# Normalising attention sums through HBM instead of by transposes, in a fused attention and FP4 feed-forward kernel

## What is computed

```
q = rope((xn @ Wqa @ Wqb).reshape(b, s, 16, 8));  k, v from xn @ Wkva @ Wkvb, k = rope(k)
scores = einsum('bqhd,bkhd->bhqk', q, k) * 8**-0.5, causal mask
w = softmax(scores);  out = einsum('bhqk,bkhd->bqhd', w, v).reshape(b, s, 128)
x + out @ Wout + bout + fp4_linear(silu(fp4_linear(xn, w_gate)) * fp4_linear(xn, w_up), w_down)
```

## Time and profile before

| | |
|---|---|
| median of 3 runs | 821.9 us (819.39 to 822.25) |
| profiled execution | 822.47 us, its span 820.7 us |
| busy: PE / DVE / ACT / POOL | 91% / 78% / 67% / 73% |
| granted TensorE clock, mean | 0.969 of full |
| DMA engines | 27.0% for the kernel's queue |

### The profile page before, as it was taken

The page is one execution under the profiler, slowest core; times in us unless marked ns, Lnnn a source line. Parts: engine busy times, 40 slices in busy tenths (PEclk is TensorE's granted clock), DMA queues, the critical chain, the costliest instruction groups (busy, mean ns, idle before and its releaser), DMA issues.

```text
span 820.7 us, 18663 instructions
## 1 busy us (share of the span) xinstructions
PE 746.0 (91%) x6641; PEld 468.1 (57%) x6733; DVE 637.2 (78%) x1396; ACT 553.2 (67%) x1169; POOL 602.6 (73%) x706
## 2 busy tenths in 40 slices
PE   2277899999999999999999999999999999999886
PEld 1143455665657565665756566666656565656444
DVE  4479788888788888888788888888887888787310
ACT  1213586777777777777777777777777777776771
POOL 5324597878879797878788797878788797856561
PEclk9668799999999999999999999999999999999997
DMA  4412323141314233241414232241413232230000
GB/s 115 124 48 77 78 75 80 54 107 50 86 45 112 58 93 76 58 111 45 98 36 109 53 105 64 63 106 50 111 49 84 47 97 60 81 75 9 21 15 14
DMA packets 66518, 58.24 MB, mean 71 GB/s; under 512 B 17554, under 2 KB 56434, under 8 KB 66426
## 3 DMA queue, kind: packets, MB, share of 16 engines
q1 hardware_dynamic: 66426, 57.04, 27.0%
HBM read 31.81 MB, written 18.61 MB: 61 GB/s over the span
## 4 chain that ended last, share of the span: by engine, by line
PE 73%; DVE 8%; ACT 6%; POOL 4%; SPq 3%; issue 3%; DMA 2%; another core or an unknown queue 0%; POOLq 0%; DVEq 0%; ACTq 0%
PE pv_ps L1038 18%; PE max_ps L1002 12%; PE exp_ps L1017 11%; PE misc_ps L1054 6%; PE max_ps L1003 6%; PE misc_ps L1103 5%; DVE neg_max L632 4%; PE misc_ps L1062 3%; PE misc_ps L1081 3%; ACT P L840 2%; PE misc_ps L1101 2%; PE misc_ps L1091 2%; PE misc_ps L1071 1%; POOL P L478 1%; PE misc_ps L1058 1%
## 5 line engine op out<-in xcount | busy, mean ns | idle before, releaser
L632 DVE TENSOR_REDUCE neg_max<-max_ps 128x1 f32<-128x512 f32 (+3 forms) x768 | 433.2, 593 | 105.2 <-PE max_ps L1003 103.6
L840 ACT ACTIVATE P<-exp_ps 128x512 f32<-128x512 f32 x512 | 293.5, 596 | 176.7 <-remote 95.5
L1017 PE MATMUL exp_ps<-Q,K 128*128 128x384 bf16 (+3 forms) x932 | 208.4, 292 | 7.5 <-ACT P L840 6.0
L1002 PE MATMUL max_ps<-K,Q 128*128 128x384 bf16 (+2 forms) x768 | 199.5, 278 | 17.2 <-DVE neg_max L632 7.0
L1003 PE MATMUL max_ps<-Kd,Q 128*128 128x128 bf16 x1024 | 190.6, 221 | 1.5 <-DVE neg_max L632 1.5
L478 POOL TENSOR_SCALAR_AFFINE_SELECT P<-P 128x512 f32<-128x512 f32 x256 | 161.7, 667 | 32.6 <-ACT P L843 32.6
L1038 PE MATMUL pv_ps<-P,V 128*32 128x512 f32 (+3 forms) x2048 | 164.2, 438 | 1.2 <-POOL P L478 0.8
L1002 PEld LDWEIGHTS max_ps<-K,Q 128*128 128x128 bf16 x768 | 75.2, 100 | 88.7 <-DVE neg_max L632 44.8
L1003 PEld LDWEIGHTS max_ps<-Kd,Q 128*128 128x128 bf16 x1024 | 99.4, 99 | 42.7 <-issue 22.8
L510 POOL TENSOR_TENSOR h<-gate_sb,up_half 128x352 f32<-128x352 f32 x64 | 59.6, 932 | 70.8 <-DVE gate_sb L645 70.8
L1017 PEld LDWEIGHTS exp_ps<-Q,K 128*128 128x128 bf16 x1024 | 82.4, 98 | 37.0 <-ACT P L840 14.3
(11 more groups left out here) (113 smaller groups left out, 1022.1 us busy)
## 6 DMA issues: line engine op xcount, KB each, us to landing
Q<-q_scr SPq DMA_DIRECT2D x64, 224.0 KB
q_scr<-q_split SPq DMA_DIRECT2D x16, 384.0 KB, 2.6
Kd<-K SPq DMA_DIRECT2D x64, 96.0 KB
x_in<-x SPq DMA_DIRECT2D x16, 256.0 KB, 5.3
q_scr<-q_split SPq DMA_DIRECT2D x16, 256.0 KB, 2.9
x_res<-x SPq DMA_DIRECT2D x16, 256.0 KB, 5.7
out<-y SPq DMA_DIRECT2D x32, 128.0 KB, 3.0
K<-k_scr SPq DMA_DIRECT2D x64, 48.0 KB
```

Of the source, the lines that this page charges most:

```text
L632: nc.vector.tensor_reduce(neg_max[:, pr // 4, i, heads[0]:heads[0] + len(heads), pr % 4], max_ps[r % 3][:, 0:len(heads) * n].rearrange("p ...
L840: nc.scalar.activation(P[g % 2][:, hh + r % 2, col:col + 512], ps[:, :], ACT.Exp, scale=SCALE).then_inc(exp_done, 1)
L1002: nc.tensor.matmul(ps[:, col:col + d], Qt, Kt[:, half, g, 0:d], start=True, stop=True)
L1017: last = nc.tensor.matmul(exp_ps[n % 2][:, col:col + width], K[par][:, half, pr // 2, kb * 128:(kb + 1) * 128], Q[par][:, pr, kb * 128:S], ...
```

## The change

The numerators and sums no longer become rows by token. SP writes `oT` (128x512, 256 KB) to HBM, and reads back two things: the sums as a compact 128x32 tile (`o_sum`), and the numerators in the layout that `onT` needs (`o_raw`, 64 partitions a half). DVE takes the reciprocals of the compact tile, SP writes them to HBM and reads them back with each repeated for the 8 rows of its head (`o_spread`). One DVE product of `o_raw` and `o_spread` in slot 5 makes `onT`. The jobs ot0, ot1 and onT leave PE, and the onT copy leaves ACT. V is laid out so that the numerators of a pair of heads are 16 rows together and the sums the next two. Some jobs change places and banks.

```diff
 MISC = [
...
-    [[("mrow1", 0, 0), ("qrot", 1, 2)], [("kk", 0, 2)], [("ot1", 1, -1)]],
+    [[("mrow1", 0, 0), ("qrot", 1, 2)], [("kk", 0, 2)], []],
     [[("gate2", 0, 1), ("up2", 1, 1)], [("v", 1, 2)], []],
-    [[("gate3", 0, 1), ("up3", 1, 1)], [("onT", 1, -1)], []],
-    [[("out0", 0, -1)], [("xqT", 1, 2)], []],
+    [[("gate3", 0, 1), ("up3", 1, 1)], [], []],
+    [[("xqT", 1, 2)], [("out0", 0, -1)], []],
     [[("out1", 0, -1)], [("mrow0", 1, 1)], []],
-    [[("ot0", 0, 0), ("hqT0", 1, 0)], [("hqT1", 1, 0)], [("hqT2", 0, 0)]],
+    [[("hqT0", 1, 0)], [("hqT1", 0, 0)], [("hqT2", 1, 0)]],
 ]
...
+            def scatter_sums(T, off, g):
+
+                if not T.has(off):
+                    return
+                T.wait(sp, oT_done, 2, off, g + 1)
+                T.wait(sp, o_sums_in, 32, off, 16 * (g + 1) - 32)
+                T.wait(sp, o_loaded, 32, off, 16 * (g + 1) - 32)
+                sp.dma_start(o_scr[g], oT[:, g, :]).then_inc(o_written, 16)
+                T.wait(sp, o_written, 32, off, 16 * (g + 1))
+
+                T.wait(sp, o_inv_done, 2, off, g - 1)
+                sums = bass.AP(tensor=o_scr[g].tensor, offset=2 * D * S, ap=[[32 * S, GH], [S, 2], [32, 16], [1, 32]])
+                sp.dma_start(o_sum[:, g, :], sums).then_inc(o_sums_in, 16)
+                T.wait(sp, o_normed, 1, off, 0)
+                raw = bass.AP(tensor=o_scr[g].tensor, offset=0, ap=[[32 * S, GH], [S, 2 * D], [1, S]])
+                sp.dma_start(o_raw[HALF * g:HALF * g + HALF, :], raw).then_inc(o_loaded, 16)
+
+            def scatter_inverses(T, off, g):
+
+                if not T.has(off):
+                    return
+                T.wait(sp, o_inv_done, 2, off, g + 1)
+                T.wait(sp, o_inv_in, 32, off, 16 * (g + 1) - 32)
+                sp.dma_start(i_scr[g], o_inv[:, g, :]).then_inc(o_inv_written, 16)
+                T.wait(sp, o_inv_written, 32, off, 16 * (g + 1))
+                T.wait(sp, o_normed, 1, off, 0)
+                inv = bass.AP(tensor=i_scr[g].tensor, offset=0, ap=[[S, 2 * GH], [0, D], [1, S]])
+                sp.dma_start(o_spread[HALF * g:HALF * g + HALF, :], inv).then_inc(o_inv_in, 16)
+
             def iteration(T):
                 if T.has(0):
...
+                scatter_sums(T, -1, 1)
+                if T.has(0):
                     place_max(T, 0, 1)
+                scatter_inverses(T, -1, 1)
...
+                scatter_sums(T, 0, 0)
                 if T.has(1):
                     place_max(T, 1, 0)
                 if T.has(-1):
                     store(T, 1)
+                scatter_inverses(T, 0, 0)
...
-            def normalize(T, off, g):
+            def invert(T, off, g):
...
-                T.misc_wait(dve, misc_filled, f"ot{g}")
-                o = misc_ps[g][:, :].rearrange("p (n s d) -> p n s d", s=2, d=16)
-                nc.vector.reciprocal(o_inv[:, :, :], o[:, :, :, D]).then_inc(o_inv_done, 1)
...
+                T.wait(dve, o_sums_in, 32, off, 16 * (g + 1))
+                T.wait(dve, o_inv_written, 32, off, 16 * (g + 1) - 32)
+                nc.vector.reciprocal(o_inv[:, g, :], o_sum[:, g, :]).then_inc(o_inv_done, 1)
+
+            def normalize(T):
...
+                T.wait(dve, o_loaded, 32, -1, 32)
+                T.wait(dve, o_inv_in, 32, -1, 32)
...
+                nc.vector.tensor_tensor(onT[:, :], o_raw[:, :], o_spread[:, :], ALU.mult).then_inc(o_normed, 1)
...
-                reduces(3, 0)
-                normalize(T, -1, 1)
-                reduces(3, 1)
+                reduces(3, 0, 1)
+                invert(T, -1, 1)
...
-                reduces(5, 0, 1, 2)
+                reduces(5, 0)
+                normalize(T)
+                reduces(5, 1, 2)
+                hidden_max(T, 3)
+                reduces(5, 3, 4)
                 output(T, 0)
-                reduces(5, 3, 4)
-                hidden_max(T, 3)
                 reduces(5, 5)
...
                 reduces(7, 2)
-                normalize(T, 0, 0)
+                invert(T, 0, 0)
                 reduces(7, 3, 4, 5)
...
-                if g == 0:
-                    T.misc_wait(act, misc_filled, "ot1")
-                else:
-                    T.prev().misc_wait(act, misc_filled, "ot0")
-                nc.scalar.activation(oT[:, :], pv_ps[:, :], ACT.Copy).then_inc(oT_done, 1)
+                T.wait(act, o_written, 32, off, 16 * (g + 1) - 32)
+                nc.scalar.activation(oT[:, g, :], pv_ps[:, :], ACT.Copy).then_inc(oT_done, 1)
```

More of the change, by code:

```diff
@@ L136, in build @@
         q_scr = [nc.dram_tensor(f"q_scr{i}", (NSLOT + 1, E, S), BF16).ap() for i in range(2)]
+        o_scr = [nc.dram_tensor(f"o_scr{i}", (128, S), F32).ap() for i in range(2)]
+        i_scr = [nc.dram_tensor(f"i_scr{i}", (128, 32), F32).ap() for i in range(2)]
         k_scr = [nc.dram_tensor(f"k_scr{i}", (3, KVH * D, S), BF16).ap() for i in range(2)]
@@ L194, in build @@
         m_row = [sb(f"m_row{i}", [16, S], BF16) for i in range(2)]
-        oT = sb("oT", [128, S])
-        o_inv = sb("o_inv", [128, NT * GH, 2])
-        o_norm = sb("o_norm", [128, NT, 2, 8, D])
+        oT = sb("oT", [128, 2, S])
+        o_sum = sb("o_sum", [128, 2, 32])
+        o_inv = sb("o_inv", [128, 2, 32])
+        o_raw = sb("o_raw", [128, S])
+        o_spread = sb("o_spread", [128, S])
         onT = sb("onT", [128, S])
@@ L268, in build @@
         oT_done = sem("oT_done")
+        o_written = sem("o_written")
+        o_sums_in = sem("o_sums_in")
+        o_loaded = sem("o_loaded")
         o_inv_done = sem("o_inv_done")
+        o_inv_written = sem("o_inv_written")
+        o_inv_in = sem("o_inv_in")
+        o_normed = sem("o_normed")
         x_res_loaded = sem("x_res_loaded")
@@ L465, in _ @@
             for i in range(2):
-                nc.gpsimd.memset(V[i][:, :, 0::2, D:D + 1], 1.0).then_inc(pool_const, 1)
-                nc.gpsimd.memset(V[i][:, :, 1::2, 16 + D:17 + D], 1.0).then_inc(pool_const, 1)
+                nc.gpsimd.memset(V[i][:, :, 0::2, 2 * D:2 * D + 1], 1.0).then_inc(pool_const, 1)
+                nc.gpsimd.memset(V[i][:, :, 1::2, 2 * D + 1:2 * D + 2], 1.0).then_inc(pool_const, 1)
             for m in (ident, ident16):
@@ L549, in iteration @@
                     for s in range(2):
-                        nc.gpsimd.tensor_copy(V[T.par(1)][:, :, s::2, 16 * s:16 * s + D],
+                        nc.gpsimd.tensor_copy(V[T.par(1)][:, :, s::2, D * s:D * s + D],
                                               v_stage[:, :, :].rearrange("p c (g d) -> p c g d", g=KVH)[:, :, s::2, :]).then_inc(v_ready, 1)
@@ L655, in hidden_max @@
                                         apply_absolute_value=True).then_inc(h_maxed, 1)
-            def normalize(T, off, g):
+            def invert(T, off, g):
                 if not T.has(off):
                     return
-                T.misc_wait(dve, misc_filled, f"ot{g}")
-                o = misc_ps[g][:, :].rearrange("p (n s d) -> p n s d", s=2, d=16)
-                nc.vector.reciprocal(o_inv[:, :, :], o[:, :, :, D]).then_inc(o_inv_done, 1)
[L664 to L671, removed]
+                T.wait(dve, o_sums_in, 32, off, 16 * (g + 1))
+                T.wait(dve, o_inv_written, 32, off, 16 * (g + 1) - 32)
+                nc.vector.reciprocal(o_inv[:, g, :], o_sum[:, g, :]).then_inc(o_inv_done, 1)
+            def normalize(T):
+                if not T.has(-1):
+                    return
+                T.wait(dve, o_loaded, 32, -1, 32)
+                T.wait(dve, o_inv_in, 32, -1, 32)
+                if T.has(-2):
+                    T.prev().misc_wait(dve, misc_filled, "out1")
+                nc.vector.tensor_tensor(onT[:, :], o_raw[:, :], o_spread[:, :], ALU.mult).then_inc(o_normed, 1)
             def output(T, n):
@@ L879, in misc_job @@
                     nc.scalar.activation(up_half[f % 2][:, :], ps[:, 0:F], ACT.Copy, scale=0.5).then_inc(misc_read[bank], 1)
-                elif job in ("xnT", "onT", "xqT") or job.startswith("hqT"):
-                    dst = {"xnT": xnT[:, :], "onT": onT[:, :], "xqT": xqT[T.par(2)][:, :]}.get(job)
+                elif job in ("xnT", "xqT") or job.startswith("hqT"):
+                    dst = {"xnT": xnT[:, :], "xqT": xqT[T.par(2)][:, :]}.get(job)
                     if dst is None:
@@ L1087, in misc_job @@
                         last = nc.tensor.transpose(rows[:, tok[c]], m_split[:, hf, c, :, :].rearrange("p s n -> p (s n)"), ident16[:, :])
-                elif job.startswith("ot"):
-                    T.wait(pe, oT_done, 2, off, int(job[-1]) + 1)
-                    for c in range(NT):
-                        last = nc.tensor.transpose(ps[:, tok[c]], oT[:, tok[c]], ident[:, :])
-                elif job == "onT":
-                    T.misc_wait(pe, misc_read, "ot1")
-                    for c in range(NT):
-                        last = nc.tensor.transpose(ps[:, tok[c]], o_norm[:, c, :, :, :].rearrange("p g n d -> p (g n d)"), ident[:, :])
```

(2 more changed lines are left out.)

## The result

The changed kernel takes 845.9 us, median of 4 runs (842.45 to 848.34), beside 820.6 (818.67 to 822.25) of the kernel before: 1.031 times the time (95% interval 1.028 to 1.034). The forecast was 845. Time, sign and the place of the new wait came out as forecast. Between the two profiled executions the difference is 22.4 us, where the forecast's sum has 22.8; but its terms did not come out: what it had for the repeating body was 5.7 us too large, what it had for the last batches and the end 4.7 too small. That the sum is right is in part luck, and what follows tells the terms apart.

What follows compares the result with a forecast made beforehand. PE bounds the kernel, busy 44.8 of a 45.6 us period. On 822.47 us: +17.5 (12 periods x 1.46), +0.5, +1.8, -2.2, -1, +6.2 at the end, total +22.8, giving 845 us; range 800 to 860.

Steps and rivals of the forecast that it cites:

- the repeating body: Periods T=0 to 13: 12 x 1.46 = 17.5 us, 0.5 more at T=0, 1.8 for T=12 and 13.
- the last batches and the end: T=14 saves 2.2 us, T=15 saves 1, the serial round trip at the very end adds 6.2.
- What holds up m_row: SP's wait for the g=0 landing delays the next batch's m_row DMAs; slot 0's first exponent tile starts 1.9 to 2.0 us later.
- So I take the queue to be served in order: SP's DMA queue: the g=0 write lands after x_in, at 448.85, bounds 445.9 and 450.0.
- What goes from PE: Three transpose groups (0.43, 0.54, 0.73 us) and slot 3's bank stall (0.53) leave PE: 2.23 us a period.
- The net per period: Each period: +2.0 us from late m_row, -0.54 from the second oT group saved before slot 3, net +1.46.
- the wait is hidden: At T=14 there are no loads, so SP's wait costs nothing and the saving stays: -2.2 us.
- costed at nothing: DVE's onT product in slot 5: 0.69 us, within 7 us spare a period; the normalisation there covered by 4 us.
- The tail: Last oT copy to first output product: copy, write, sums, reciprocal, write, spread, product in a row, 10.4 us, so +6.2.
- The signs named ahead: Changed profile: periods about 47.1 us, slot 0 m_row waits 3 to 4, g=0 landing over 5, slot 7 DVE wait 2 to 3.
- Rival A: At SP's wait behind x_in, the write is not held up, lands at 445.9; period -1.6 us, total 803; chance 0.22.
- its better corner: Even m_row is hidden at slot 0, so all 2.2 us a period stay: 795 us.

Runs made afterwards that it cites:

- run 5: The changed kernel with the g=0 write of oT issued by ACT on ACT's own DMA queue instead of SP's: 843.9 us, 1.029 times the kernel before.
- run 4: The changed kernel without its ten DMAs a batch, reciprocals and onT made from constant tiles, normalised attention output left out: 803.5 us, 0.981 times the kernel before.
- run 9: The changed kernel with the m_row DMAs issued right behind the wait for the g=0 landing, ahead of the two reads: 852.7 us, 1.038 times the kernel before.
- run 1: The kernel before, plus a 256 KB write to HBM behind the x_in load, awaited before the four m_row DMAs: 823.2 us, 1.006 times the kernel before.
- run 2: The changed kernel with the hf=0 m_row DMAs issued between the g=0 write of oT and the wait for its landing: 820.6 us, 1.002 times the kernel before.
- run 3: On top of run 2, the g=0 reciprocals and their way through HBM moved from slot 7 to the next body: 819.3 us, 0.999 times the kernel before.
- run 5b: The changed kernel with the x_in load issued behind the hf=0 m_row DMAs instead of ahead of the oT write: 826.6 us, 1.009 times the kernel before.
- run 6: On top of run 3, two of DVE's block maxima (hidden_max 2 and 3) moved a slot later: 819.4 us, 1.000 times the kernel before.
- run 7: Run 3 with the last batch alone normalised by transposes as in the kernel before: 809.4 us, 0.988 times the kernel before.
- run 8: Run 6 and run 7 together, with DVE's second h_mag operation behind two more reduces in slot 4: 811.5 us, 0.987 times the kernel before.

## Why the prediction was right, and where its steps failed

**What holds up m_row: right.** Forecast for T=7, from the x_in issue to PE's first tile of slot 0: 10.8 us. Measured: from 448.34 to the weight load at 459.57, 11.2. In the mean of T=1 to 11 this stretch is 9.4 us before and 11.4 after, +2.0 as forecast. The write's landing was put 5.7 us behind its issue and took 5.1; the read issues 1.0, measured 1.3; the start of the last `m_row` issue to PE's go 1.6, measured 2.3. "So I take the queue to be served in order" named the wrong place, although it priced the landing well: on ACT's queue the write takes as long (run 5). It is the work already given to the DMA engines that is left as the cause.

**"What goes from PE": the size that failed.** 2.23 us a period were forecast, 0.93 went (run 4). Of the onT group's 0.73 nothing, since the distance to the next row held DVE's lag as well as the transposes; of slot 3's 0.53 stall 0.31; and slot 5 lost 0.31, because two exponent tiles now come sooner than ACT can take them. The oT groups were right, 0.45 and 0.50 for 0.54 and 0.43. The distance to the next row was taken as the cost of a group, and what would have held that next row anyway was not asked. In the sum it stands whole only at T=14 (-2.2). In the repeating body it sets how long PE waits, not how long the period is.

**The net per period: the part pulled forward was too small.** There the period is the length of a chain: PE's start of slot 0, the x_in issue, the landing, `m_row`, the next start. The forecast had +2.0 for the stretch behind the x_in issue and -0.54 for the one ahead of it, 1.46. The stretch ahead, from the first exponent weights of slot 0 to the x_in issue, takes 35.6 to 36.9 us before, 36.3 in the mean of T=1 to 11, and 35.3 after (in the nine of these periods whose clock stayed up): -1.0. Of this 0.8 is there already at the q_scr issue (T=7, before and after, with 429.49 in the earlier trace rows):

```profile
405.86 0.10 PEld L1017 LDWEIGHTS exp_ps<-Q,K 128*128 128x128 bf16 x1
```

```profile
413.26 0.10 PEld L1062 LDWEIGHTS exp_ps<-Q,K 128*128 128x128 bf16 x1 [1.52 <-issue]
...
436.12 1.55 SPq L467 DMA_DIRECT2D q_scr<-q_split  x3
```

429.49 - 405.86 = 23.63 before, 436.12 - 413.26 = 22.86 after, that is the second oT group's 0.45 and the 0.31 of slot 3's stall, which the forecast had counted as saved too late. So a period grows by 1.95 - 1.04 = 0.9 in those nine, and by 0.6 in the one shown above. PE's wait is what is left of it: 46.31 less its own 44.75 makes 1.56, where 1.62 was read.

**What made up for it.** For T=0 to 13 the sum has 17.5 + 0.5 + 1.8 = 19.8 us, and 14.1 were measured. In this are two things that were not forecast: three times the wait was longer, 2.3 to 2.7 us, and behind two of these the clock fell; those two periods alone give 5.8 of the 14.1 us (48.42 and 48.73 against 45.68). The last two batches were to save 3.2 us and cost 0.3. For T=14 "the wait is hidden" holds for `m_row`, but PE then waits for DVE's product in slot 5, which was costed at nothing and takes three times as long there as in the periods before (the last section comes back to it); T=13 has the same wait, of 1.17. T=14:

```profile
768.11 0.46 PE L1138 MATMUL misc_ps<-wout_sb,onT 128*128 128x128 f32 x2 [1.29 <-DVE onT L718]
```

**The tail: right in kind, 1.2 us too small.** Forecast 10.4 us from the last copy to the first output product, +6.2; measured 832.20 - 820.55 = 11.65, against 4.2, +7.4:

```profile
820.55 0.60 ACT L902 ACTIVATE oT<-pv_ps 128x512 f32<-128x512 f32 x1 [3.41 <-PE pv_ps L1083]
821.18 0.31 SPq L427 DMA_DIRECT2D o_scr<-oT  x1
823.18 0.54 SPq L432 DMA_DIRECT2D o_sum<-o_scr  x1
...
825.25 0.35 DVE L707 RECIPROCAL o_inv<-o_sum 128x32 f32<-128x32 f32 x1 [11.39 <-DMA o_sum<-o_scr]
825.63 0.32 SPq L443 DMA_DIRECT2D i_scr<-o_inv  x1
828.12 0.60 SPq L447 DMA_DIRECT2D o_spread<-i_scr  x1
831.36 0.69 DVE L718 TENSOR_TENSOR onT<-o_raw,o_spread 128x512 f32<-128x512 f32 x1 [5.76 <-DMA o_spread<-i_scr]
832.20 0.77 PE L1138 MATMUL misc_ps<-wout_sb,onT 128*128 128x128 f32 x2 [11.71 <-DVE onT L718]
```

From row to row: the 256 KB write 2.0 (2.7 forecast), the sums 2.1 (1.9), the small write of the reciprocals 2.5 (1.8), the spread read 3.2 (1.9). The way of the reciprocals, a write of 16 KB and the read that repeats them over 64 partitions of 512, was priced too low; the forecast had taken it from landings in the body (k_scr 1.6, q_scr 2.7).

**The signs named ahead.** Wait for `m_row` at each slot 0: there, but 1.2 to 2.7 us and not 3 to 4, since PE gained 1.3 us less and the period grew less. Periods of 47.1: mostly 46.2 to 46.7. The g=0 write over 5 us: 5.1 in T=7, 5.2 in the median of T=0 to 11. One of these landed in 3.5 us (T=10), and the interval behind it is the shortest of the thirteen, 45.8. A DVE wait of 2 to 3 us before the reciprocal: 0.4 in T=7. Rival A is excluded by that landing, and its better corner by run 4: even without any transfer the kernel takes 803.5, where A had 795 for everything hidden.

**What stays open.** Which engines the Q loads keep busy, and so why the write needs 5 us while the mean share is low, was not measured. Nor was the slow product of T=13 and 14 tried by itself, nor traced which of the other executions of the kernel before kept the full clock in the tail.

## What to carry to other kernels

Before pricing what leaves the busiest engine, ask at that very place how far the next engine is behind: here the transposes stood partly in time that PE would have waited anyway, and a kernel that leaves the new path out showed the ceiling (1.9%, of which the tail is a good part) in one run. Where one queue issues everything in order, a wait for a landing belongs behind every DMA that somebody needs soon, though run 9 shows that what is moved behind must not be needed sooner still; moving it behind `m_row` and taking the reciprocal a body later turned 3% slower into no change. And a round trip through HBM that is hidden in the body is paid in full at the end: doing the last batch the old way made the change 1.2% faster than the kernel before.

## What the runs showed of the hardware

**The clock after a stall.** PE waited 1.62 us at 459.8, and its four gate and up products then took 1.35 us (row above) at full clock. At T=9 it waited 2.71:

```profile
507.21 0.35 PE L1047 MATMUL max_ps<-K,Q 128*128 128x384 bf16 x1 [2.71 <-DMA Q<-m_row]
...
507.89 2.55 PE L1099 MATMUL misc_ps<-wguT,xqT 128*128 128x352 f32 x4
```

Busy time and clock of the stall and of the stretch behind it:

```profile
504.40:507.10 2.70, 0.11 (x2) 0.13 (x2) 0.73 (x2) 0.00 (x0) 1.33 (x3) 1.00 0.27 75
507.20:510.40 3.20, 3.19 (x8) 1.84 (x8) 1.72 (x4) 2.18 (x5) 0.24 (x1) 0.53 0.30 82
```

PE did almost nothing for 2.7 us, and behind that the granted clock was 0.53, nearly the lower level (1.2 of 2.4 GHz), for 3.2 us: the same four products took about twice as long, 1.2 us more. The wait of 2.29 us at T=3 did the same (clock 0.55 in the 3.2 us from 227.2). The length of the stall does not decide alone: behind a wait of 2.51 us at T=12 (648.33) the granted clock was 1.00, and so it was behind the others of this trace, 1.15 to 1.93 us. In run 9 it fell behind waits of 1.97 (T=7 and, to 0.61, T=9) and 2.74 us, and not behind those of 2.00, 2.03 and 2.65. What decides stays open; so in a forecast of a new stall of about 2 us or more, a fall of the clock behind it belongs into the upper end.

**The clock in the tail.** From the first output product to the end the kernels run the same 32 matmuls. The kernel before, run 1 and the change:

```profile
809.85:820.60 10.75, 7.54 (x32) 6.95 (x32) 0.85 (x2) 0.00 (x0) 0.00 (x0) 0.61 0.09 24
813.34:820.70 7.36, 4.07 (x32) 3.69 (x32) 0.85 (x2) 0.00 (x0) 0.00 (x0) 1.00 0.12 36
832.20:843.00 10.80, 7.54 (x32) 6.95 (x32) 0.85 (x2) 0.00 (x0) 0.00 (x0) 0.50 0.09 26
```

At the full clock this stretch is 3.4 us shorter. Where PE stood still for over 11 us ahead of it (the change and runs 2, 3, 5, 5b, 6 and 9) it took 10.9 us each time; with the transposes at the end it took 7.4 (runs 1 and 7), 9.0 (run 8) and, in the profiled execution of the kernel before, 10.85. So the 7.4 us that the tail costs in the change are counted against an execution whose own tail was slow; against the tail of run 1, 11.2 us, they would be 11.3.

**A DVE product three times as long.** Of the 16 `onT` products 13 take 0.73 us or less, those of the bodies T=13 and T=14 take 2.04, that of T=15 1.33. DVE and POOL in slot 5 of T=8, the product first:

```profile
488.54 0.72 DVE L718 TENSOR_TENSOR onT<-o_raw,o_spread 128x512 f32<-128x512 f32 x1
...
488.68 3.31 POOL L532 TENSOR_TENSOR h<-h,h_mag 128x1408 f32<-128x1408 f32 x1
```

and at T=13, POOL first, since it has no statistics of a later batch to do ahead of it:

```profile
722.97 2.04 DVE L718 TENSOR_TENSOR onT<-o_raw,o_spread 128x512 f32<-128x512 f32 x1
...
721.61 2.85 POOL L532 TENSOR_TENSOR h<-h,h_mag 128x1408 f32<-128x1408 f32 x1
```

Whichever starts later takes longer: POOL's 3.31 for 2.85, DVE's 2.04 for 0.72. The product at T=13 ends at 725.01, 0.55 us after POOL's end at 724.46, most of its usual length. Without the other, each is short: in the kernel before, which has no such product, POOL's operation takes 2.85 to 2.87 in all 16 batches, and the last product of the change, with POOL idle, takes 0.69. Run 4 has 2.04 too, with no transfer of the sums at all, so it is not the DMAs. The Trainium skill, "SBUF — State Buffer", section "Who interferes with whom", states that a DVE instruction with two SBUF inputs contends with a GpSimd instruction that reads SBUF, and that the order of issue decides which of the two is held up. Both orders of this trace agree; no run moved one of the two by itself.
